# Block transposes on VectorE with four stores each, in place of transposes on TensorE, in a three-layer graph kernel

## The reference

```python
edge_index = jnp.stack([src, dst])
h = jnp.maximum(_layernorm(x, axis=-1), 0.0)
x = x + _L0_gnn_ref(h, edge_weight, L0_gnn_bias, edge_index)   # h @ W.T + bias, W sparse, 1024 x 1024
h = jnp.maximum(_layernorm(x, axis=-1), 0.0)
x = x + _L1_gnn_ref(h, src, dst, ...)                          # two SAGE layers

def _sage_layer(h, edge_src, edge_dst, deg_inv, W_self, W_neigh, b):
    msg = h[edge_src]
    agg = jax.ops.segment_sum(msg, edge_dst, num_segments=h.shape[0])
    mean = agg * deg_inv[:, None]
    return h @ W_self + mean @ W_neigh + b
# _L1_gnn_ref: h = relu(sage(x, ..0)); out = sage(h, ..1)
```

## Time and profile before

| | us |
|---|---|
| median of 3 runs | 776.24 (773.78 to 777.6) |
| the profiled execution | 780.45 |
| its span on the core | 778.7 |
| TensorE busy | 751.2 (96%) |
| VectorE, GpSimd, ScalarE busy | 573.7, 477.8, 354.3 |
| mixing ends, dense products of layer 0 | from about 210 |
| products with A in layer 0 | 414 to 502 |
| dense products of layer 1 | 503 to 694 |
| products with A in layer 1 | 694 to 775 |

### The profile page before, as it was taken

How to read it: one execution, slowest core, us unless ns; L and a number is a source line. 1 busy time by engine, 2 the same in 40 slices (tenths; PEclk the granted TensorE clock), 3 DMA queues, 4 the chain that set the end, 5 groups by cost and what they waited for, 6 DMA issues and landing times.

```text
span 778.7 us, 13499 instructions
## 1 busy us (share of the span) xinstructions
PE 751.2 (96%) x4433; PEld 621.5 (80%) x4434; DVE 573.7 (74%) x813; ACT 354.3 (46%) x596; POOL 477.8 (61%) x593
## 2 busy tenths in 40 slices
PE   2999999999899999999999999999999999999997
PEld 2878878888778888888888888888888888887886
DVE  7999687788445799986768785446487958579885
ACT  7867633334244257642335655543222323244731
POOL 5000256757658899777756292327699966745982
PEclk9999999999989999999999999999999999999999
DMA  3123367565375763475864625686753668785475
GB/s 115 43 79 102 115 193 256 194 227 183 122 275 173 268 218 106 151 236 183 307 233 148 203 95 162 220 255 228 256 163 126 212 227 285 243 272 186 153 235 196
DMA packets 82873, 148.78 MB, mean 191 GB/s; under 512 B 10795, under 2 KB 20898, under 8 KB 82800
## 3 DMA queue, kind: packets, MB, share of 16 engines
q1 hardware_dynamic: 62862, 105.07, 42.5%
q10 hardware_dynamic: 19938, 42.79, 15.4%
HBM read 106.42 MB, written 41.41 MB: 190 GB/s over the span
## 4 chain that ended last, share of the span: by engine, by line
PE 79%; POOL 9%; issue 6%; DMA 2%; DVE 2%; POOLq 2%; ACT 1%; SPq 0%; DVEq 0%; ACTq 0%
PE bank L1717 50%; PE bank L1767 21%; POOL AT L1062 9%; PE bank L1544 4%; DMA az<-asum_scratch 1%; PE bank L1534 1%; POOLq L1062 1%; PE bank L1783 1%; PE bank L1555 1%; PE bank L1561 1%; POOLq L630 1%; DMA dst_g<-in_dst 0%; DMA stage<-hT_scratch 0%; DVE R L1935 0%; DVE L L1950 0%
## 5 line engine op out<-in xcount | busy, mean ns | idle before, releaser
L1717 PE MATMUL bank<-slot,split 128*128 128x512 f32 x1128 | 264.1, 393 | 4.7 <-issue 4.7
L1717 PEld LDWEIGHTS bank<-slot,split 128*128 128x128 f32 x1128 | 212.5, 189 | 49.1 <-issue 5.1
L1062 POOL TENSOR_TENSOR AT<-AT,az 128x50 int32 (+3 forms) x288 | 96.4, 335 | 118.6 <-DMA az<-asum_scratch 71.6
L1717 PE MATMUL bank<-slot,split_third 128*128 128x512 f32 x552 | 129.6, 390 | 0.3 <-DVE cst L2316 0.3
L1717 PEld LDWEIGHTS bank<-slot,split_third 128*128 128x128 f32 x552 | 103.1, 188 | 22.0 <-DVE cst L2316 0.5
L1767 PE MATMUL bank<-slot,Ax 128*128 128x512 f32 x500 | 118.9, 392 | 0.2
L2087 DVE TENSOR_TENSOR slot<-T,slot 128x512 fp32r<-128x512 f32 x64 | 85.3, 1349 | 34.1 <-ACT slot L1320 31.3
L1767 PEld LDWEIGHTS bank<-slot,Ax 128*128 128x128 f32 x500 | 92.8, 188 | 20.3 <-issue 1.4
L1651 PE MATMUL bank<-slot,split_m 128*128 128x512 f32 x320 | 91.1, 396 | 0.0
L1117 POOL TENSOR_TENSOR T<-T,wst 128x512 f32<-128x512 f32 x48 | 66.8, 1409 | 2.4 <-DMA wst<-in_L_gnn_W_self 2.2
L1651 PEld LDWEIGHTS bank<-slot,split_m 128*128 128x128 f32 x320 | 58.5, 188 | 11.0
(11 more groups left out here) (229 smaller groups left out, 1197.8 us busy)
## 6 DMA issues: line engine op xcount, KB each, us to landing
stage<-hT_scratch SPq DMA_DIRECT2D x90, 256.0 KB, 3.7
wst<-in_L_gnn_W_neigh SPq DMA_DIRECT2D x56, 256.0 KB, 4.8
wst<-in_L_gnn_W_self SPq DMA_DIRECT2D x56, 256.0 KB, 3.2
x1b_scratch<-x ACTq DMA_DIRECT2D x10, 512.0 KB, 5.2
hT_scratch<-hTs ACTq DMA_DIRECT2D x10, 512.0 KB, 3.1
wst<-prod0g_scratch SPq DMA_DIRECT2D x20, 256.0 KB, 3.0
hT_scratch<-h1s ACTq DMA_DIRECT2D x20, 256.0 KB, 3.2
wst<-prod1g_scratch SPq DMA_DIRECT2D x20, 256.0 KB, 2.8
```

The source lines that it names most:

```text
L1062: pool.tensor_tensor(a, a, az32[:, n % NZ, pairs * pos:pairs * (pos + 1)], ALU.add) \
L1717: last = pe.matmul(dense_bank(v, which)[:, :], split_tile(v, a)[:, NT * k:NT * (k + 1)], slot[t % 2][:, b, HF * (HK * which + k):HF * (HK ...
```

## The change

- In layer 0 the output tile no longer goes to TensorE. VectorE transposes it in one instruction, in blocks of 32 by 32, from `cst` into a ring of NH = 3 (`h1s` and a third tile), in the step after its own. ScalarE applies the ReLU in place and issues four stores (NB = 4), each of 32 partitions by 4 pieces of 128 elements, so that the blocks change places on the way. VectorE's transpose of tile o waits for the four stores of tile o - 3.
- What arrives in SBUF has another order within a partition; in layer 1 `operand_hi` and `operand_lo` read it in runs of 32 elements and write the split operand in the old order.
- `hT_d` is laid out by halves; the second norm's result is still transposed by TensorE.
- Of GpSimd's 21 additions in the last slot of the mixing, 14 stay ahead of `operand_lo(0)`, 7 move behind it.
- `count_edges` runs at v = 7, 8, 9 and 19 to 25 in place of 8 to 17; `degrees` and `turn` two products later; AT_TOP is 29 in place of 22.
- The last output tile is taken and stored in two halves, one store issued by ScalarE, one by SyncE.

```diff
+B = 32
+NB = NT // B
+NH = 3
+LAST_ADDS = 2 * MIX_ADDS // 3
-FIRST_DEG = 8
-AT_TOP = 22
+COUNTED_AT = [7, 8, 9, 19, 20, 21, 22, 23, 24, 25]
+SUMMED_UP = {v + 2: k for k, v in enumerate(COUNTED_AT)}
+AT_TOP = 29
...
+        def by_block(half):
+            return half.rearrange("p (k c f) -> p c k f", k=HK, c=NB)
+        def turned_blocks(half):
+            return half.rearrange("p (c k n) -> p c k n", c=NB, k=HK)
+        def h1_tile(o):
+            r = o % NH
+            return h1s[:, r, :] if r < 2 else more_sums[:, r - 2, :]
+        def by_nodes(tile):
+            return tile.rearrange("p (a k n) -> p a k n", a=NB, k=HK)
+        def by_rows(tile):
+            return tile.rearrange("p (k a n) -> p a k n", a=NB, k=HK)
...
+        def store_last(eng, half):
+            u, column, n = OUTS[OL - 1]
+            eng.wait_ge(s_res, 2 * OL + half)
+            at = HF * column + LAST * half
+            eng.dma_start(out[NT * n:NT * n + rows_of(n), at:at + LAST],
+                          res_tile(OL - 1)[0:rows_of(n), LAST * half:LAST * (half + 1)]).then_inc(...)
...
-            for slot_of_adds in range(TN + 1):
+            for slot_of_adds in range(TN):
                 add_asums(slot_of_adds)
+            add_asums(TN, last=LAST_ADDS)
...
             operand_lo(0)
+            add_asums(TN, first=LAST_ADDS)
             operand_lo(1)
...
+                if v < VL:
+                    pool.tensor_tensor(split_tile(v, 1), source(v), high, ALU.subtract).then_inc(s_olo, 1)
+                else:
+                    pool.tensor_tensor(by_rows(split_tile(v, 1)), by_nodes(source(v)), by_rows(high),
+                                       ALU.subtract).then_inc(s_olo, 1)
...
+                if layer == 0:
+                    act.copy(split_tile(v, 0), source(v)).then_inc(s_ohi, 1)
+                else:
+                    act.copy(by_rows(split_tile(v, 0)), by_nodes(source(v))).then_inc(s_ohi, 1)
...
-                if o >= 2:
-                    act.wait_ge(s_h1d[o % 2], used(o - 2, 2))
-                act.activation(h1s[:, o % 2, :], bank[6 + o % 2][:, 0:HK * NT], ACT.Relu).then_inc(s_h1, 1)
+                act.activation(h1_tile(o), h1_tile(o), ACT.Relu).then_inc(s_h1, 1)
                 act.wait_ge(s_h1, o + 1)
-                act.dma_start(hT_d[1][n][:, HK * half:HK * (half + 1), :].rearrange("p k n -> p (k n)"),
-                              h1s[:, o % 2, :]).then_inc(s_h1d[o % 2], 16)
+                for a in range(NB):
+                    act.dma_start(hT_d[1][n][half].rearrange("(c f) n -> f c n", c=NB)[:, :, P * a:P * (a + 1)],
+                                  h1_tile(o)[B * a:B * (a + 1), :].rearrange("p (c n) -> p c n", c=NB)) \
+                        .then_inc(s_h1d[o % NH], 16)
...
-            def turn_res(o):
-                pe.wait_ge(s_res, o + 1)
-                if o >= 2:
-                    pe.wait_ge(s_h1, o - 1)
-                for k in range(HK):
-                    last = pe.transpose(bank[6 + o % 2][:, NT * k:NT * (k + 1)], res_tile(o)[:, P * k:P * (k + 1)],
-                                        ident[0:NT, 0:NT])
-                last.then_inc(s_t2, 1)
...
+            def turn_res(o):
+                dve.wait_ge(s_res, o + 1)
+                if o >= NH:
+                    dve.wait_ge(s_h1d[o % NH], turned_stored(o - NH, NH))
+                dve.transpose(turned_blocks(h1_tile(o)), by_block(res_tile(o))).then_inc(s_t2, 1)
...
                 for u in range(VL):
+                    if layer == 0 and u - 1 in OUT_AT:
+                        turn_res(OUT_AT[u - 1])
```

More of the change, by code:

```diff
@@ L158, in build_program @@
                for which in "gs"] for layer in range(2)]
-    hT_d = [nc.dram_tensor(f"hT{layer}_scratch", (TN, P, KT, NT), F32, kind="Internal").ap() for layer in range(2)]
+    hT_d = [nc.dram_tensor(f"hT{layer}_scratch", (TN, 2, P, HK * NT), F32, kind="Internal").ap() for layer in range(2)]
     with ctx:
@@ L440, in build_program @@
         s_h1 = sem("s_h1")
[L441 removed]
+        s_h1d = [sem(f"s_h1dram{i}") for i in range(NH)]
         s_out = [sem(f"s_out{i}") for i in range(NO)]
@@ L872, in load_sums @@
                 if o == 0 and layer == 1:
-                    for r in range(2):
-                        sp.wait_ge(s_h1d[r], used(OL - 2 + r, 2))
+                    for last in range(OL - NH, OL):
+                        sp.wait_ge(s_h1d[last % NH], turned_stored(last, NH))
                     for i in range(TN - 2, TN):
@@ L1047, in _, with add_asums @@
             a_bases = []
-            def add_asums(slot):
-                for j, c in adds_in(slot):
+            def add_asums(slot, first=0, last=None):
+                for j, c in adds_in(slot)[first:last]:
                     n, pos = UNIT_OF[(j, c)]
@@ L2315, in take @@
                 dve.wait_ge(s_ag, VL * layer + u + 1)
+                if layer == 1 and o == OL - 1:
+                    for half in range(2):
+                        part = slice(LAST * half, LAST * (half + 1))
+                        dve.scalar_tensor_tensor(out=res_tile(o)[:, part], in0=ps[:, part], scalar=dinv[:, n:n + 1],
+                                                 in1=sums_tile(layer, o)[:, part], op0=ALU.mult, op1=ALU.add) \
+                            .then_inc(s_res, 1)
+                    return
                 dve.scalar_tensor_tensor(out=res_tile(o), in0=ps, scalar=dinv[:, n:n + 1], in1=sums_tile(layer, o),
                                          op0=ALU.mult, op1=ALU.add).then_inc(s_res, 1)
+            def turn_res(o):
[3 more added lines that the diff above has]
+                dve.transpose(turned_blocks(h1_tile(o)), by_block(res_tile(o))).then_inc(s_t2, 1)
             def products_of_A(layer, heavy):
```

43 lines of the change are left out of this document (20 added, 23 removed).

## The result

| | us |
|---|---|
| kernel before, median of 5 runs | 775.9 (773.78 to 777.6) |
| changed kernel, median of 5 runs | 784.86 (783.02 to 786.59) |
| ratio | 1.013 (95% interval 1.0111 to 1.0149) |
| profiled execution of the changed kernel, its span | 786.59, 784.9 |

The changed kernel is slower by 1.3%; the two medians stand 9.0 us apart. The forecast was 778.4 with a range of 770 to 787: the time lies inside and the direction was right, but only 2.2 us of the rise were forecast, a quarter of it.

A forecast was written before the change was run, and what follows sets the result against it. TensorE was taken as the bound, busy 751.2 of 778.7 us. Terms of 4.7 (net half layer), 2.5 (clock), -4.5 (start) and -0.5 (end) gave +2.2 on the 776.24 median: 778.4 us, range 770 to 787.

The forecast's parts named there:

- Part 1: Second half of layer 0: 20 groups of transposes leave TensorE, 8.8 us less if nothing else becomes the path.
- Part 2: VectorE in layer 0: 20 block transposes of 128x512 at 0.7 us each, bounds 0.69 and 1.78, just fitting its step.
- Part 3: ScalarE in layer 0's second half: four issues per tile add 1.4 us, making that half net 4.7 us slower.
- Part 4: Joint of layers 0 and 1: TensorE stands some 4 us, its clock halves, 2.5 us lost.
- rival 2: Joint of layers 0 and 1: the clock does not fall, total 775.9 us; chance 12%.
- Part 5: Start of the dense products: seven GpSimd additions move behind the first low part, 4.5 us gained (1.5 to 5).
- Rival 4: Start gives only 2.5 us or less, as the clock falls anyway or products wait for GpSimd: 781 us; chance 12%.
- Part 6: End of the kernel: last result made and stored in two halves on two queues, 0.5 us gained (0 to 1).
- Part 7: Layer 1: ScalarE's casts and GpSimd's subtractions read in runs of 32, at no cost.
- Rival 3: Layer 1: GpSimd becomes the bound, each subtraction dearer by half from reading in runs: 784.1 us; chance 18%.
- Rival 1: ScalarE's issues are cheap or run beside its work, so the 8.8 us stay gained: 762.4 us; chance 10%.

The follow-up runs named there:

- the exchange on the loads: Changed kernel with one whole store per tile on ScalarE, blocks exchanged by SyncE's four loads per tile in layer 1, and five turned tiles in the ring: 769.82 us.
- ring of five: Changed kernel with five places in place of three for the turned tiles, stores still issued by ScalarE: 783.9 us, ratio 1.0128.
- the second profile of before: The kernel before, unchanged, profiled once more: 774.37 us, span 772.6.
- cut store: The kernel before with only its layer 0 tile store cut in pieces: four of 32 partitions 785.2 us, two of 64 partitions 776.33 us.

## Why the prediction was right or wrong

The measure is the stretch between the marks, the start before them and the end behind them.

**Part 1 (transposes, -8.8): right.** With the exchange on the loads the stretch takes 88.0 us against 95.2: 7.2 of the 8.8 arrive, and 0.8 and 1.5 us stand in two pauses, one at step 24 (for VectorE) and one at the joint (for the operand from ScalarE and GpSimd).

**Part 2 (block transpose 0.7 us): right.** A row of VectorE in the changed kernel (busy us, mean ns | idle before and what ended it):

```profile
L2363 DVE STREAM_TRANSPOSE h1s<-cst 128x512 f32<-128x512 f32 x14 | 9.9, 710 | 11.2 <-DMA hT_scratch<-h1s 11.0
```

It takes 710 ns, near the lower of my bounds. The estimate of 1.24 us for four squares, worked out from the 311 ns that the Trainium skill ("VectorE: DVE Perf Modes", the three transpose paths) gives for a 128x128 of 2-byte elements, was too high for this form. I had charged nothing for the 0.7 us on VectorE; the pause of some 0.8 us in front of step 24, for a sum of VectorE, stands in all nine traces with block transposes (0.72 to 0.85) and in none of those that transpose on TensorE. Whether VectorE's added work causes it, or TensorE only comes there sooner, is not shown.

**Part 3 (ScalarE's issues, net +4.7): the mechanism right, the size too small.** Four issues take 1.77 to 1.88 us in 15 of 20 tiles (forecast 1.79), the step 3.77 (3.7). The two terms:
- From the end of step 25 to the first product of layer 1 I had 33.0 us; it took 36.3 (471.29 to 507.55). The chain there runs through ScalarE's list, as I had counted it. The chain at the joint:

```profile
499.61 0.62 ACT slot L1363
500.23 0.54 ACT h1s L1478
...
505.17 0.63 ACT split_third L1375
...
505.93 1.28 POOL split_third L1141
```

  At the end of step 25 ScalarE was 0.85 us behind already (its next copy started at 472.14; I had 0), the seven full steps took 28.0 (25.9), the two tiles 5.0 (4.9), the cast, the low part and the start 2.4 (2.3). 1.5 of the 3.2 missing are one tile's issues, in which a single one took 2.00 us where the others take 0.46.
- Before it, to the end of step 25, I had charged 1.5 us of waiting, as an estimate of how far ScalarE falls behind the ring. It was 4.8: from the first mark to the end of step 25 it took 64.7 us, before 63.4 with 3.5 us of transposes in it. The rows show 1.03, 0.66, 1.66 and 0.83 in front of steps, 4.2 together (the 0.83 is the one for VectorE); the rest lies in gaps too small for a row. This term was the worst of the half layer: I worked out one place (steps 11 and 12) and took it for the only one. ScalarE is late in others too, as here, where the four issues of tile 1 take 3.46 us and the next copy comes straight behind them, while TensorE waits 1.03:

```profile
426.48 3.46 ACTq L1481 DMA_DIRECT2D hT_scratch<-h1s  x4
430.04 1.35 ACT L1420 CAST Ax<-s 128x640 fp32r<-128x640 int16 x2 [3.58 <-PE bank L1814]
```

That VectorE's new wait costs nothing of its own was right for this kernel (ring of five), and no longer so when ScalarE is relieved.

**Part 4 (the clock, +2.5): right.** I had one pause, behind step 34. There were two, one ahead of step 34 as well, and both the step (2.4 us longer) and the product (2.3) ran at half clock. Only the product counts: step 34 ends at 503.8, and the first product waits until 507.55 for ScalarE's list. In the ring of five step 34 ran at full clock and the product came no sooner for it. So the clock cost 2.3 us of the time, and rival 2 (no fall of the clock) is out.

**Part 5 (the start, -4.5): wrong, it is 0.** This is the step that failed. The 4.66 us of pause and the half clock in the earlier trace rows belong to the profiled execution and not to the kernel; I had noted that it was 4.2 us above the median and then took the 4.2 off at the end and the 4.5 off in the sum. It is the same time, taken off twice. Rival 4 named the smaller gain, for other reasons. The part of it that was to come from the clock leaned on a pause of 2.2 us being too short for a fall; a pause of 2.16 us in another kernel was followed by a step at half clock (4.13 us). The edit may help in those executions where GpSimd is late, which these runs are too few to show: the ten runs with it alone lie between 772.72 and 774.57, the fifteen of before beside them between 772.75 and 779.93, at the same median.

**Part 6 (the end, -0.5): no gain found.** From TensorE's last matmul to the end of the span it is 3.9 to 4.4 us in six traces with one store, 3.4 to 4.8 in eight with two halves. The half-microsecond is below what these show.

**Part 7 (reads in runs of 32, 0): right.** GpSimd's subtraction of a loaded operand takes 1366 ns on average in layer 1 (1379 over both layers before), ScalarE's cast 621 (624), and layer 1 is as long as it was (265.1 us behind the second mark, 265.4 before). Rival 3 is out.

```profile
L1141 POOL TENSOR_TENSOR split<-stage,split 128x512 fp32r<-128x512 f32 x16 | 21.8, 1366 | 19.0 <-ACT split L1375 19.0
```

**The sum.** The forecast was 6.5 us too low. Take the second profile of before (774.37, without the late start) and the changed kernel's (786.59): 12.2 us apart, 2.2 forecast, 10.0 missing. 6.3 of it lie in the stretch (3.3 before the end of step 25, 3.2 behind it, 0.2 the other way for the clock), 3.3 at the start (4.5, less the 1.2 by which the changed kernel's first mark stands ahead, 406.62 against 407.81) and 0.5 at the end. Two differences between executions then hid a third of the miss: the profiled execution of the changed kernel lies 1.7 above its median, and the 776.24 from which I started 1.9 above 774.37. The time fell inside the range because the range was wide enough for the issues to cost more; that is partly luck and no proof of the sum. Of the rivals, the first (issues cheap) is refuted. The kernels that take the issues away reach 766.7 to 772.4, where it had forecast 762.4 with the same false 4.5 in it.

**The signs named beforehand** came: four issues of 1.6 to 1.9 us, Ax copies straight behind block casts, TensorE waiting for ScalarE in steps 31 to 33 (I had said 30 to 34), a block transpose near 0.7, a pause of over 3 us at the joint with the clock halved. GpSimd's subtraction kept its median of 1.29 us. The one that did not come is the first product at 213.4: it came at 211.

## What to carry over

Cost a DMA issue as an instruction of the engine that issues it, and add it to that engine's list for a step before anything else: here a list of 2.3 us against TensorE's 2.75 took one more issue for 1.5 us and three more for 10. Cut a transfer into pieces on the side whose issuer has time, and look what else stands in that issuer's list behind a store that waits. Before a pause in a trace is counted as a gain, compare the profiled execution's own time with the median: if it lies above it by about the length of the pause, the pause may be that difference.

## What the hardware did that I had not expected

- A store of 128 partitions takes 0.33 us of ScalarE's queue, two of 64 partitions 1.10 (0.45 and 0.61 each), two of 32 partitions 0.84, four of 32 partitions 1.73 to 1.88 in most tiles, with pieces of 2 KB (cut store) or 512 B (exchange) nearly alike. The price goes neither with the bytes nor with the size of the pieces: each further issue in a row costs more than the one whole store. Why two of 64 partitions take longer than two of 32 is open. The Trainium skill ("DMA: Bandwidth & Descriptors", the anatomy of one DMA) has about 50 ns for the sequencer's part of a DMA that GpSimd issues. Rival 1 took that figure over for ScalarE, where it does not apply: on ScalarE's queue in the changed kernel the least is 309 ns. The row of 56 of its issues (duration in ns: min/median/max, then first and last start in us):

```profile
L1481 ACTq DMA_DIRECT2D hT_scratch<-h1s x56: 309/460/2135, 421.9 to 517.0; - x56
```

- Now and then one issue takes 1 to 2 us. In the chain of the changed kernel:

```profile
496.53 2.00 ACTq L1481
498.56 0.46 ACTq L1481
```

  In all five kernels with block transposes and four stores it fell on tile 1 (2.61 to 3.46 us for its four issues; 1.84 in the kernel with its store cut in four), in two on tile 14 (3.32 and 3.03). The two kernels with the cut store have one each elsewhere (1.3 and 1.0 us), those with one store for a tile have none. The cause is open: no experiment was made for it.
- A pause of TensorE of 2.39 us, and one of 2.56 in another kernel, left the clock at its full 2.4 GHz; one of 2.16 us in a third was followed by a step at 1.2 GHz (4.13 us for ten matmuls). Behind every pause of 3.5 us and more after the mixing, in all traces here, matmuls ran at half clock. The length of a pause between 2.1 and 2.9 us alone does not tell.
- GpSimd's additions end up to 6 us apart from one execution to another with the same order of them (208.11, 210.17 and 214.44 for the start of the low part). Much of GpSimd's idle time before additions ends with a load of what it adds (71.1 of 110.6 us on the changed kernel's page); why the loads come sooner or later is open.
